# Image attention in another order with zero products; down weights requested by GpSimd; two units moved ahead of the routed tiles; transposed router logits

## The reference

```
img = layernorm(patches @ patch_w) + sinusoidal_pe        # 8 x 64 tokens
x   = attn64(ff(img)) + img;  x = ff(x) + x               # 12 heads of 16, window 64
txt = layernorm(word[ids] + domain[ids2] @ proj_w.T + kind + pos)   # 8 x 128 tokens
h   = concat(x, txt)                                      # 8 sequences of 192 tokens
z   = ln(h); a = window_attention(z); s = linear_attention(z)
h   = h + (a + ln(s)) @ out_w;  h = h + gelu(ln(h) @ w1) @ w2
y   = ln(h)                                               # 1536 tokens
p   = softmax(y @ gate_w.T); the two best of 16 experts, weights renormalised
h   = h + sum_k weight_k * expert_k(y) + mean of 2 shared experts(y)
expert(y) = (silu(y @ wg) * (y @ wu)) @ wd                # 192 -> 768 -> 192
```

## Time and profile before

| what | value |
|---|---|
| three timed runs | 831.49, 820.0, 818.48 us |
| the profiled execution, device time | 815.28 us |
| its span, first to last instruction | 813.6 us |
| PE matmuls busy | 768.3 us (94%) |
| DVE / ACT / POOL busy | 297.7 / 242.9 / 190.4 us |
| mean granted TensorE clock | 0.962 of full speed |
| HBM read and written | 90.65 MB and 9.83 MB |
| chain that ended last, by engine | PE 81%, DVE 10%, issue 4%, ACT 2%, ACT's queue 2% |

### The profile page before, as it was taken

One profiled execution on the slowest core, in us unless ns is written; L12 is line 12 of the kernel. 1 busy time (PEld: TensorE's weight loads), 2 busy tenths in 40 slices (PEclk: granted clock), 3 DMA queues, 4 the chain that ended last, 5 costly groups with the idle time before them and its releaser, 6 DMA issues.

```text
span 813.6 us, 16603 instructions
## 1 busy us (share of the span) xinstructions
PE 768.3 (94%) x6686; PEld 534.9 (66%) x6686; DVE 297.7 (37%) x781; ACT 242.9 (30%) x514; POOL 190.4 (23%) x246
## 2 busy tenths in 40 slices
PE   8999799889999899899899989989999999999998
PEld 7446545556666657667447565478788778878455
DVE  1337346555636546534231562211111111111233
ACT  0112423545455464444231301112222221222111
POOL 5524215462221313310010035200000000000362
PEclk9898699999999999889898999999999999999999
DMA  9500000900000000000000024189999999995132
GB/s 331 202 0 2 3 0 1 327 5 3 2 1 2 2 2 2 2 2 2 1 0 1 1 101 165 58 285 336 343 361 346 326 362 339 356 326 198 35 87 64
DMA packets 31947, 101.33 MB, mean 125 GB/s; under 512 B 4729, under 2 KB 18062, under 8 KB 26384
## 3 DMA queue, kind: packets, MB, share of 16 engines
q1 hardware_dynamic: 21616, 67.71, 22.8%
q10 hardware_dynamic: 5760, 23.60, 8.4%
q0 software_dynamic: 4512, 9.19, 3.5%
HBM read 90.65 MB, written 9.83 MB: 124 GB/s over the span
## 4 chain that ended last, share of the span: by engine, by line
PE 81%; DVE 10%; issue 4%; ACT 2%; ACTq 2%; POOL 0%; DVEq 0%; POOLq 0%
PE PS L1498 13%; PE PS L2190 8%; PE PS L2078 8%; PE PS L2092 5%; PE PS L2194 5%; PE PS L2080 4%; PE PS L2206 3%; PE PS L2162 2%; PE PS L1504 2%; PE PS L1771 1%; PE PS L2211 1%; PE PS L1787 1%; DVE sm L1253 1%; PE PS L1560 1%; PE PS L1848 1%
## 5 line engine op out<-in xcount | busy, mean ns | idle before, releaser
L1459 DVE TENSOR_TENSOR rh<-rsg,PS 128x768 f32<-128x768 f32 x32 | 30.5, 954 | 166.9 <-ACT rsg L929 166.9
L2190 PE MATMUL PS<-xt,w_rgu 128*128 128x128 f32 x576 | 71.1, 278 | 5.6 <-ACT xt L908 5.6
L2190 PEld LDWEIGHTS PS<-xt,w_rgu 128*128 128x128 f32 x576 | 67.0, 192 | 10.4 <-ACT xt L908 8.4
L2078 PE MATMUL PS<-X,w_sgu 128*128 128x512 f32 x144 | 72.0, 624 | 0.1
L622 POOL DMA_DIRECT2D y_slots<-ys x32 | 17.4, 542 | 231.5 <-ACT ys L915 231.5
L929 ACT ACTIVATE rsg<-PS 128x768 f32<-128x768 f32 x32 | 26.0, 811 | 133.8 <-PE PS L2194 103.0
L2092 PE MATMUL PS<-w_sdn,gu 128*128 128x192 f32 x288 | 48.8, 329 | 2.5 <-DVE acc L1349 2.3
L2092 PEld LDWEIGHTS PS<-w_sdn,gu 128*128 128x128 f32 x288 | 46.6, 190 | 6.9 <-issue 3.8
L1498 PE MATMUL PS<-w_rdn,rh 128*128 128x192 f32 x288 | 50.9, 327 | 0.0
L767 ACT ACTIVATE pb<-sm,nm 128x128 f32<-128x128 f32 x144 | 42.2, 371 | 25.2 <-DVE nm L1257 25.1
L2078 PEld LDWEIGHTS PS<-X,w_sgu 128*128 128x128 f32 x144 | 25.2, 193 | 36.0 <-issue 34.2
(11 more groups left out here) (369 smaller groups left out, 1429.5 us busy)
## 6 DMA issues: line engine op xcount, KB each, us to landing
w_rgu<-in_wgu SPq DMA_DIRECT2D x24, 1152.0 KB, 8.3
w_pgu<-in_wgu SPq DMA_DIRECT2D x16, 1152.0 KB, 8.6
w_rdn<-in_wd ACTq DMA_DIRECT2D x24, 576.0 KB, 5.2
w_pdn<-in_wd ACTq DMA_DIRECT2D x16, 576.0 KB, 5.6
x_slots<-zeros SPq DMA_DIRECT2D x1, 3072.0 KB, 19.4
xs<-x_slots SPq DMA_DIRECT2D x32, 96.0 KB, 4.6
y_slots<-ys POOLq DMA_DIRECT2D x32, 96.0 KB, 6.5
w_sgu<-in_shared_gu SPq DMA_DIRECT2D x2, 1152.0 KB
```

Source lines behind the costliest of these rows:

```text
L1459: dve.tensor_tensor(rh[:, j, :], rsg[:, j, :], PS[:, 2:4, :].rearrange("p a b -> p (a b)")[:, 0:FF], ALU.mult).then_inc(S["r_h"], 1)
L2078: pe.matmul(PS[:, 2 * c + n % 2, :], w_sgu[:, e, c, cols_m], x[:, c, :], start=True, stop=False)
L2190: pe.matmul(dst(y, m), w[:, y, 128 * m:128 * m + 128], xt[:, j, y, :], start=(m % 4 == 0), stop=False, skip_group_check=True)
```

## The change

Six edits. (1) Image attention: the bias of the projection and the values go ahead of the scores; turned weights of tile 2 use PSUM banks 2 and 3, turned outputs banks 0 and 1; 18 products of ones and zeros (`spare`, 128 x 192, results never read) stand at places where PE waits; DVE's and ACT's lists are reordered to fit, and GpSimd clears `va`, `sm` and `pb` ahead of the last text rows. (2) 12 more such products in the first and the last pair (q = 0: 3 and 4; q = 3: 3 and 2). (3) The router's logits are computed transposed: the gate (padded to 32 columns) is stationary, three 128-token groups go to three column groups of the array; ACT copies the rows to `gates`, PE turns them back. (4) The third down tile of chunk 0 goes ahead of the count products. (5) Units 24 and 25 (BEFORE = 2) go ahead of the routed tiles, with their products in a buffer of their own. (6) ACT requests the first two down weights only; GpSimd requests all others, for tile i+4 right after it has stored tile i.

```diff
+BEFORE = 2
 SCORE_BANK = (0, 4, 0, 0)
+TURNED_BANK = (4, 4, 2, 4)
...
+        def product(k, m):
+
+            return early[:, m, :] if k == EARLY and m < BEFORE else gu[:, k % 2, m, :]
...
                     sp.wait_ge(S["e_dn"], 4 * EARLY)
+                    sp.wait_ge(S["e_gu"], FM * EARLY + BEFORE)
                     load_weights(0, FR)
...
-            text_gain(6)
-            text_gain(7)
-            norm_power(0, 2, first_half)
 
             pool.wait_ge(S["t_pm"], 4)
             pool.wait_ge(S["a_mm"], 2 * HG)
...
             ins.then_inc(set_up, 1)
+
+            text_gain(6)
+            text_gain(7)
+            norm_power(0, 2, first_half)
...
+            def load_down(r, k):
+                for h, at in enumerate(slots_of(r, k)):
+                    e = pool.value_load(expert[0:1, at], min_val=0, max_val=E_R - 1)
+                    pool.dma_start(down_weights(k, h), a["wd"][bass.ds(e, 1)].rearrange("o p c n -> p (o c) n")).then_inc(S[f"r_d{k}"], 16)
+
+            pool.wait_ge(S["d_slot"], 2)
+            pool.wait_ge(S["r_y"], 2)
+            for k in range(2, RK):
+                load_down(0, k)
+
             def store(i, n, j, r, k):
                 pool.wait_ge(S["r_ye"], i + 3)
                 pool.dma_start(y_tiles[rows_of(r, k)].rearrange("o p d -> p o d"), ys[:, j:j + 1, :]).then_inc(S[f"r_st{j}"], 16)
+                if not isinstance(i, int) or i + RK < RT:
+                    load_down(r + 1, k)
...
+            image_values_out(0)
+            image_values_out(1)
             image_exponents(0)
             image_exponents(1)
-            image_values_out(0)
-            image_values_out(1)
+            image_weights_out(0)
             image_exponents(2)
-            image_weights_out(0)
             image_weights_out(1)
             image_exponents(3)
+            image_weights_out(2)
             outputs_out(0)
-            image_weights_out(2)
             outputs_out(1)
             image_weights_out(3)
...
+            def gates_out(n, bank, at):
+                act.wait_ge(S["c_lg"], n + 1)
+                act.activation(gates[:, at], PS[0:HS * TP, bank, 0:at.stop - at.start], ACT.Copy).then_inc(S["c_go"], 1)
+
             table_of(ACT.Gelu, 9)
             gelu(p)
+            gates_out(0, 4, slice(0, 128 * p))
             table_of(ACT.Silu, 10)
             silu(7, 8)
             inputs_turned(p)
             silu(9, 9)
+            gates_out(1, 5, slice(128 * p, 128 * PAIRS))
             table_of(ACT.Exp, 11)
             act.wait_ge(S["c_ls"], 1)
             act.activation(lg[:, :, :], lg[:, :, :], ACT.Exp).then_inc(S["c_ex"], 1)
             table_of(ACT.Silu, 12)
-            silu_loop(10, (EARLY * FM - 10) // 2)
+            silu_loop(10, (EARLY * FM + BEFORE - 10) // 2)
...
-                if not static or i + 2 < RT:
-                    act.wait_ge(S["r_y"], i + 1)
-                    load_down(r + (k + 2) // RK, (k + 2) % RK)
...
+            dve.wait_ge(S["a_pb"], 2)
+            dve.tensor_tensor(pb2[:, :], PS[:, 4:6, VB0], cols[:, COLS["tok_proj_b"]:COLS["tok_proj_b"] + 2], ALU.add
+                              ).then_inc(S["a_pb"], 1)
             text_sums(6, 7)
             norm_apply(in_h, in_acc, first_half, 0, "p_rs1", "p_x")
             image_queries(2)
-            dve.wait_ge(S["a_pb"], 2)
-            dve.tensor_tensor(pb2[:, :], PS[:, 4:6, VB0], cols[:, COLS["tok_proj_b"]:COLS["tok_proj_b"] + 2], ALU.add
-                              ).then_inc(S["a_pb"], 1)
             less_maximum(0)
+            text_norms(6, 7)
             less_next_maximum(1)
             less_next_maximum(2)
-            text_norms(6, 7)
-            dve.wait_ge(S["p_x"], B // 2)
-            norm_statistics(in_acc, first_half, "p_ve2")
+            image_outputs(0)
             less_next_maximum(3)
-            image_outputs(0)
             image_outputs(1)
             image_outputs(2)
             image_outputs(3)
-            norm_apply(in_acc, z_in, first_half, 0, "p_rs2", "p_z")
+            dve.wait_ge(S["p_x"], B // 2)
+            norm_statistics(in_acc, first_half, "p_ve2")
...
+            gate_times_up(FM * EARLY, FM * EARLY + BEFORE - 1)
...
+            def spare(bank, n):
+
+                for _ in range(n):
+                    pe.matmul(PS[:, bank, 0:D], ones_sq[:, :], zeros[:, :], start=True, stop=True)
...
+                    proj_bias()
                     text_terms(3)
                     pe.wait_ge(S["a_q"], 1)
                     pe.wait_ge(S["a_k"], 1)
                 in_pairs(w_tqk, g, y1T, (2 * g) % 4, (2 * g) % 4 + 1, "a_mm")
...
             def img_scores(i):
                 if i == 1:
-                    pe.wait_ge(S["a_pb"], 3)
-                    pe.wait_ge(S["t_rd"], B)
+                    pe.wait_ge(S["a_v"], 2)
...
+            pe.wait_ge(S["a_pb"], 3)
+            img_values()
+            pe.wait_ge(S["a_q"], HG)
+            pe.wait_ge(S["a_k"], HG)
             img_scores(0)
+            pe.wait_ge(S["t_rd"], B)
+            spare(7, 5)
             img_scores(1)
+            pe.wait_ge(S["a_sub"], 1)
+            spare(0, 4)
             img_scores(2)
             pe.wait_ge(S["a_sub"], 2)
-            img_values()
             img_turn_weights(0)
+            spare(7, 3)
+            img_outputs(0)
             img_scores(3)
-            img_outputs(0)
             img_turn_weights(1)
+            pe.wait_ge(S["a_on"], 1)
+            spare(7, 2)
+            img_outputs(1)
+            pe.wait_ge(S["a_sub"], IT)
+            img_turn_weights(2)
             img_turn_outputs(0)
-            img_outputs(1)
-            img_turn_weights(2)
             img_turn_outputs(1)
+            spare(7, 1)
             img_outputs(2)
             img_turn_weights(3)
             img_turn_outputs(2)
+            spare(7, 1)
             img_outputs(3)
+            pe.wait_ge(S["a_ptc"], IT)
+            spare(4, 2)
             img_turn_outputs(3)
...
+                    else:
+                        pe.wait_ge(S["so_read"], q)
+                        spare(7, 3)
                     turn_tiles(in_z, "c_z1", p, "z1_mm")
...
+                    if q == 0 and j == 1:
+                        spare(7, 3)
+                    elif q == PAIRS - 1 and j == 3:
+                        pe.wait_ge(S["x2_read"], q)
+                        spare(7, 2)
...
+                    if q == 0 and j == 2:
+                        pe.wait_ge(S["fold_v"], 1)
+                        spare(7, 4)
...
-            def logits(first, last):
-                for t in range(first, last + 1):
-                    mm = accumulate(PS[:, 4, E_R * t:E_R * t + E_R],
-                                    [(X[:, 0, 128 * t:128 * t + 128], w_gate[:, 0, :]),
-                                     (X[DR:DM, 1, 128 * t:128 * t + 128], w_gate[DR:DM, 1, :])])
+            def gate_rows(pairs, bank):
+                for rows, c in ((slice(0, 128), 0), (slice(DR, DM), 1)):
+                    for n, pair in enumerate(pairs):
+                        for k in range(TP):
+                            at = PT * pair + 128 * k
+                            mm = pe.matmul(PS[HS * k:HS * k + HS, bank, 128 * n:128 * n + 128], w_gate[rows, c, :], X[rows, c, at:at + 128],
+                                           start=(c == 0 and n == 0), stop=(c == 1), skip_group_check=True)
+                mm.then_inc(S["c_lg"], 1)
+
+            def turn_gates(pairs, n):
+                pe.wait_ge(S["c_go"], n + 1)
+                for pair in pairs:
+                    mm = pe.transpose(PS[:, 4, HS * TP * pair:HS * TP * (pair + 1)], gates[:, 128 * pair:128 * pair + 128],
+                                      ident[0:HS * TP, 0:HS * TP])
                 return mm
...
-            logits(0, TP * p - 1)
+            gate_rows(range(p), 4)
             narrow(p)
             up_units(7, 8)
+            turn_gates(range(p), 0)
             turn_tiles(lambda t: h_sb[:, normal_at(TP * p + t), :], "c_x3", p, "c_x3T")
             up_units(9, 9)
             pe.wait_ge(S["c_x3s"], PAIRS)
-            logits(TP * p, NT - 1).then_inc(S["c_lg"], 1)
+            gate_rows([p], 5)
+            turn_gates([p], 1).then_inc(S["c_lg"], 1)
             up_units(10, 11)
             down_tiles(0, (0, 1))
+            pe.wait_ge(S["c_ls"], 1)
+            down_tiles(0, (2,))
             pe.wait_ge(S["d_m"], 1)
             for k, w in enumerate((earlier, ones_sq)):
                 pe.matmul(PS[:, 6, NT * E_R * k:NT * E_R * (k + 1)], w[:, :], mask[:, :, :].rearrange("p t e -> p (t e)"),
                           start=True, stop=True).then_inc(S["d_cnt"], 1)
-            down_tiles(0, (2, 3))
+            down_tiles(0, (3,))
             down_tiles(1, range(4))
             for k in range(2, EARLY):
                 up_units(FM * k, FM * k + FM - 1)
                 down_tiles(k, range(4))
+            up_units(FM * EARLY, FM * EARLY + BEFORE - 1)
             pe.wait_ge(S["e_acc"], 4 * EARLY)
```

(15 more changed lines are left out.)

69 lines of the change are left out of this document (35 added, 34 removed).

## The result

In 20 alternating runs of each the changed kernel takes 812.64 us (809.26 to 818.7) and the kernel before 821.61 (812.38 to 831.49). The ratio is 0.9937, with a 95% interval of 0.9908 to 0.9966: 5 us faster, 3 to 8. The ratio leaves out the long runs of the kernel before (four lie over 1.5% above its fastest), so it says less than the 9 us between the two medians. The profiled execution has a device time of 810.25 us and a span of 808.7, where the one of before had 815.28 and 813.6.

What follows compares the result with a forecast made beforehand. PE was taken to carry the chain nearly everywhere: its rows, short waits and half-clock stretches. Terms summed to -5.95 us, 809.3 from the profiled execution, 814.0 from the median; 811 was taken between, range 801 to 824.

Steps and rivals of the forecast that it cites:

- Image attention: New order, zero products and separate PSUM banks in the image attention: -6.0 us, bounds -7.9 and 0.
- Zeros in the end pairs: 12 zero products in first and last pair: three ahead of a shorter wait, others cost nothing; +0.4 us.
- Rival B: Zeros and shift also spare later clock falls, at slices 17 and 18 (325 to 366 us): 5 less, 806; chance 0.20.
- Logits: Three pairs' transposed logits: -3.7 us with the turn back; narrow layer behind at full clock: -2.6, or 0.
- Routing: Third down tile ahead of the counts: PE's wait for DVE's add grows to 4.3 us, ends 1.3 later; +1.3.
- Units: Two units ahead of the routed tiles: +5.95 us, tail gives nothing back; later start of first routed tile: +1.6.
- Rival A: The tail does shrink, because gathers or DVE's adds have unseen slack: 6 us less, 805; chance 0.10.
- Tokens behind three queues: At the routed tiles' start, three loaded queues stretch SP's transfer and delay tile 2's tokens: +1.3 us, bounds 0 and 3.
- Routed tiles: With down requests on GpSimd, `xt` is ready 1.5 us sooner in the routed tiles: -4.2 us.
- rival D: Routed rounds do not get shorter, because transfers are the bound: +4 us, 815; chance 0.10.
- Rival C: Idle at the counts, first routed tile and tail lowers the clock, up to 3.4 us each: +10, 821; chance 0.20.
- Rival E: Zero products do not hold the clock in the image attention, cost 0.6 us each: +6 to +8, 818; chance 0.10.

Runs made afterwards that it cites:

- clears_mid: The changed kernel with GpSimd's clears between the last two text rows and the norm of the first half; 805.71 us, ratio 0.9811 to the kernel before.
- best: The changed kernel with clears between text rows and norm, third down tile behind the counts, BEFORE = 0; 792.80 us, ratio 0.9649 to the kernel before.
- zeros_out: The changed kernel without its 30 zero products, those at the program's start kept; 823.33 us, ratio 1.0015 to the kernel before.
- best_logits_old: `best` with the router's logits computed as before the change; 800.00 us, ratio 0.9791 to the kernel before.
- units_back: The changed kernel with BEFORE = 0, the two units returned to the tail; 805.94 us, ratio 0.9806 to the kernel before.
- fill_idle: The changed kernel with more zero products in waits at the counts, the first routed tile and the tail; 807.50 us, ratio 0.9817 to the kernel before.
- counts_back: The changed kernel with the third down tile behind the count products again; 807.63 us, ratio 0.9827 to the kernel before.
- first set: Four kernels sharing runs of before: the changed kernel again, clears behind the last text rows, `units_back`, `counts_back`; medians 816.16, 813.86, 805.94, 807.63 us.

## Why the prediction was right or wrong, point by point

**Image attention: wrong, and the largest error.** Forecast -6.0 (bounds -7.9 and 0), measured +0.55. The step that failed is one sentence, "GpSimd's clears ran beside PE before and do so now: nothing." I had asked what the clears do to PE, and not what they do to DVE, which they had met before only while it read PSUM. What the runs showed in its place: four rows of DVE 4.4 us longer, PE idle for 2.60 us ahead of the first scores, and half clock behind that. The order itself was laid out well enough: with the clears out of the way (`clears_mid`) the projection begins at 92.74 us, 7.0 before the changed kernel's, and the clock is 1.00 from 62 to 106. The stretch of the table's second line is then 6.7 us shorter than before the change (36.4 against 43.1), between the -6.0 forecast and the bound of -7.9, and the 1.9 us that I gave back for the projection were not lost (1.99 us for its first four rows).

**Zeros in the end pairs: wrong in sign.** +0.4 forecast, -3.1 measured for the pairs between the two profiles, and 7 to 10 us when the twelve are taken out of the best version (10 in the pairs of `zeros_out` too). The sentence that failed is that those standing in waits "cost nothing": I had priced them as work in a wait, and given the clock behind the wait no term. By the rows of `zeros_out` they carry all of the change's gain. Rival B, with 0.20, had the mechanism and half the size: both dips that it named (slices 17 and 18) are gone.

**Logits: right.** 6.46 to 1.64 us, 4.8 and not the 4.1 that I took off: 46 ns a row, nearer the 50 of four column groups than the 67 that I took. The narrow layer at full clock: -2.63 measured, -2.6 forecast, and `best_logits_old` shows the tie.

**Routing: right in the wait, short in the clock.** The wait grew from 2.32 to 4.28 us (4.3 forecast) and ended 1.9 later, of which 0.4 had been won at the last pair's logits. What came on top is 1.7 us of half clock behind it.

**Units: right.** +5.95 and +1.6 forecast, +7.3 measured; the tail gave nothing back, PE stood idle 1.72 and 3.92 us in it, where 1.9 and 4.1 were forecast. Rival A is out: `units_back` shows a tail of 53.0 us with two units more.

**Tokens behind three queues: not seen.** The +1.3 were never paid in the changed kernel's two profiles, for the first tile at half clock took longer than the tokens were late; where the clock stays up, PE waits for `xs`, 0.82 us in `fill_idle` and 2.15 in `clears_mid`, inside the bounds of 0 and 3. The working itself had a hole: 15.2 less 13.4 is 1.8 and not 1.3. And the wait is not only the units' doing: with BEFORE = 0 it is 1.19 us in `units_back` and 1.53 in `best`.

**Routed tiles: right, a little small.** -4.2 forecast, 5.2 us in seven rounds; rival D is out.

**Rival C: the mechanism true, the price 6.0 and not 10.** All three idle stretches were followed by a fall in the profiled execution: 1.7, 2.5 (5.46 against 2.94 us for the first routed 24 rows) and 0.3 (1.88 against 1.61 for the rows behind them) at the routed tiles, 1.5 in the tail (7.97 against 6.44), 6.0 together, where up to 3.4 each was put down. I had made it a case of its own with 0.20. It belonged in the sum, beside B, for the two are one mechanism: what zero products give, idle takes. Rival E was half right: in the changed kernel the first nine zero products of the image attention did run at half clock, 0.72 us each (3.57 and 2.93 us for 18 rows), and the 18 together gained 2.4 us at most; but from 86 us on the clock was 1.00 with them, and 0.50 without.

**The number.** 811 was forecast for the median and 812.64 measured, inside the range 801 to 824. But what was forecast was a change of -9 from the 820 shown, and the ratio says -5 (-8 to -3); between the medians of all runs it is -9. The change is as small as it is for two reasons that the runs separate: the clears (some 8 us by `clears_mid`) and the two units with the third down tile (8.7 and 3.6 us in the rows of `units_back` and `counts_back`). The first was in no term of the sum; the second was, but for the clock that falls behind the idle it opens, 6.0 us in the profiled execution. That these came near to cancelling against the 10 us of the zero products in the pairs was luck.

**Left open.** All four kernels of the first set waited 1.7 to 2.6 us once, at 499 to 511 us, because ACT began a silu late that PE had long made ready; no other profile has such a wait. Its cause is not known.

## What to carry to other kernels

When work moves on a helper engine, look at what every other engine does in the new interval, not only the one on the critical path: a clear that cost nothing beside reads of PSUM stopped VectorE for 4.4 us beside rows from SBUF to SBUF. Where TensorE waits 2 to 4 us, the wait can cost half as much again in clock behind it (1.7 us behind 4.3, 1.6 and 2.5 behind 2.9), and a few zero products in it can be worth more than their time. Take them out again place by place: here 12 of the 30 carried all of the gain. The worst is to open such a wait by moving work off the place. Before moving work ahead of a stage, ask what bounds the place it comes from: out of a tail bound by a chain of gathers nothing is saved.

## What the runs showed of the hardware

- Beside GpSimd's memsets in SBUF, DVE's `tensor_scalar` rows from SBUF to SBUF did not end until the last of a row of memsets was done (four rows 5.63 us where they take 1.24; 4.13 us where a tile of 128 x 4 takes 0.17). Passes that read PSUM were not held up (0.96 and 0.96 us), nor was `BATCH_NORM_AGGREGATE` from SBUF to SBUF (0.28 us).
- The granted clock fell behind idle of 2.9 to 4.3 us at each of three places in both profiles of the changed kernel; behind idle of 2.15 to 2.9 us in other kernels it fell in some (2.31 us in `best`, 2.15 in `clears_mid`) and not in others (2.32 in `counts_back`, 2.89 in `clears_mid`). It also fell behind 36 rows with a moving side of only 16 columns, with no idle at all (narrow layer 8.76 against 6.12 us).
- Two executions of one kernel differed in span by 7.4 us (808.7 and 816.1): 2.6 us of it was one wait more, the rest clock (0.979 and 0.971).
